# Input turned whole, one block of programs, and shifted half rows moved by DMA in a two-part attention kernel

## The reference

```
y = causal linear attention of layernorm(x)      # 16 heads of 8, rope, elu + 1
x = x + layernorm(y Wo)
z = layernorm(x)
for l in 0, 1:
    h = shift(z);  q, k, v = split(h wqkv[l])       # 8 heads of 64
    q, k = rope(l2norm(q) qs), rope(l2norm(k) ks)
    z = z + local_attention(q, k, v) wo[l]          # windows of 64, own and previous
    h = layernorm(shift(z)) g + b
    z = z + (a * gelu(g)) w2[l] + b2[l]             # a, g = split(h w1[l] + b1)
out = x + layernorm(z)

shift(t): features 0..63 of a token stay; features 64..127 come from the token before (0 for the first)
```

## Time and profile before

| | |
|---|---|
| median of 3 runs | 1832.37 us (1830.87 to 1837.6) |
| profiled execution | 1839.22 us |
| its span, first to last instruction | 1836.7 us |
| mean granted clock of TensorE | 0.971 |
| busy: PE, DVE, ACT, POOL | 1641.0, 1329.3, 1367.3, 1285.8 us |
| chain that ended last: PE, ACT, POOL, issue, DVE | 70, 12, 7, 6, 3 % |
| loads of x_in | issued at 35.7, 87.5, 172.7, 273.7, 377.9, ... 1523.3 us |

### The profile page before, as it was taken

One profiled execution on the slowest core, in us unless ns is written; L12 is line 12 of the kernel. 1 busy time (PEld: TensorE's weight loads), 2 busy tenths in 40 slices (PEclk: granted clock), 3 DMA queues, 4 the chain that ended last, 5 costly groups with the idle time before them and its releaser, 6 DMA issues.

```text
span 1836.7 us, 51372 instructions
## 1 busy us (share of the span) xinstructions
PE 1641.0 (89%) x18212; PEld 1149.2 (63%) x18340; DVE 1329.3 (72%) x3471; ACT 1367.3 (74%) x4277; POOL 1285.8 (70%) x1715
## 2 busy tenths in 40 slices
PE   0677989999999999999999999999999999998875
PEld 0344666666667666666666666666667666666653
DVE  2465777877777787877778787777777787776552
ACT  1264768787887878798887878787787878788663
POOL 1263777777777887777777787777777887777562
PEclk9888999999999999999999999999999999999986
DMA  3000001011111011111111011111101011111001
GB/s 117 12 16 19 22 23 25 18 36 30 36 28 28 19 34 27 31 36 30 36 28 28 19 31 30 31 36 28 39 22 31 22 25 36 30 31 30 19 21 29
DMA packets 58135, 54.52 MB, mean 30 GB/s; under 512 B 7538, under 2 KB 42780, under 8 KB 57756
## 3 DMA queue, kind: packets, MB, share of 16 engines
q1 hardware_dynamic: 57884, 51.25, 11.0%
HBM read 13.48 MB, written 8.39 MB: 12 GB/s over the span
## 4 chain that ended last, share of the span: by engine, by line
PE 70%; ACT 12%; POOL 7%; issue 6%; DVE 3%; DMA 0%; POOLq 0%; ACTq 0%; DVEq 0%; SPq 0%
PE bank L732 10%; PE bank L787 7%; PE bank L759 7%; PE bank L798 5%; PE bank L744 5%; PE bank L771 5%; PE bank L838 4%; PE bank L827 4%; PE bank L679 4%; PE bank L695 3%; PE bank L753 2%; PE bank L719 2%; ACT probs L959 2%; ACT probs_t L853 2%; POOL qk_rows L1308 2%
## 5 line engine op out<-in xcount | busy, mean ns | idle before, releaser
L959 ACT ACTIVATE probs<-bank,s_low 128x128 f32<-128x128 f32 x1024 | 360.1, 384 | 60.7 <-DVE s_low L1171 60.6
L1308 POOL TENSOR_TENSOR qk_rows<-qk_rows,qk_tmp 128x512 f32<-128x512 f32 x256 | 328.2, 1282 | 16.6 <-DVE qk_tmp L1159 15.8
L1321 POOL TENSOR_TENSOR probs<-probs,s_rden 128x512 f32<-128x512 f32 x256 | 263.5, 1050 | 68.1 <-DVE s_rden L1180 68.1
L732 PE MATMUL bank<-wqkv_sb,h_cols 128*128 128x512 f16 x1152 | 281.2, 388 | 7.9 <-ACT probs_t L853 2.6
L1311 POOL TENSOR_TENSOR qk_rows<-qk_rows,qk_rnorm 128x512 f32<-128x512 f32 x256 | 268.7, 1050 | 20.1
L959 ACT ACTIVATION_READ_ACCUMULATOR probs<-bank,s_low 128x1 f32 x1024 | 229.0, 224 | 0.0
L1156 DVE TENSOR_TENSOR qk_rows<-bank,rope 128x512 f32<-128x512 f32 x256 | 174.4, 681 | 39.2 <-POOL qk_rows L1311 35.4
L1126 DVE TENSOR_TENSOR room<-bank,const 128x512 f32<-128x512 f32 x256 | 158.7, 683 | 57.8 <-PE bank L679 56.2
L732 PEld LDWEIGHTS bank<-wqkv_sb,h_cols 128*128 128x128 f16 x1152 | 108.2, 99 | 142.7 <-issue 22.7
L853 ACT ACTIVATE probs_t<-bank 128x512 f32<-128x512 f32 x256 | 140.9, 598 | 67.9 <-PE bank L771 65.2
L1142 DVE TENSOR_REDUCE qk_sum<-qk_sq 128x16 f32<-128x1024 f32 x128 | 155.1, 1212 | 46.2 <-ACT qk_sq L918 44.2
(11 more groups left out here) (154 smaller groups left out, 3650.6 us busy)
## 6 DMA issues: line engine op xcount, KB each, us to landing
v_even<-v_rows SPq DMA_DIRECT2D x224, 128.0 KB, 2.3
x_in<-in_L_attn_x SPq DMA_DIRECT2D x16, 256.0 KB, 3.2
kept_rows<-x_in SPq DMA_DIRECT2D x16, 256.0 KB, 2.3
x_back<-kept_rows SPq DMA_DIRECT2D x16, 256.0 KB, 3.0
out<-x_back SPq DMA_DIRECT2D x16, 256.0 KB, 2.4
room<-in_constants SPq DMA_DIRECT2D x1, 1024.0 KB
hidden<-in_L_ffn_wqkv SPq DMA_DIRECT2D x1, 768.0 KB
qk_rows<-in_L_ffn_wqkv SPq DMA_DIRECT2D x1, 768.0 KB
```

What stands on the lines that cost most here:

```text
L732: mm = pe.matmul(to[:, :], h_cols[st.l][:, x_half, st.j * P:(st.j + 1) * P], wqkv_sb[:, st.l, w_half, w * INNER:(w + 1) * INNER], start=(n ...
L959: act.activation(probs[st.l][:, n, :], bank[b[half]][:, c * P:(c + 1) * P], ACT.Exp, bias=s_low[st.l][:, a, n:n + 1], accum_out=s_sum[st.l ...
L1308: pool.tensor_tensor(rows(w), rows(w), qk_tmp[l][:, w, :], ALU.add).then_inc(pool_qk.of(st), 1)
L1321: pool.tensor_tensor(probs[l][:, mine, :], probs[l][:, mine, :], s_rden[l][:, a, mine].unsqueeze(2).to_broadcast([P, PAIRS, P]), ALU.mult) ...
```

## The change

1. **h**: PE makes four whole transposes of 128 features. ACT and DVE each write in two instructions: partitions 0 to 63 straight, partitions 64 to 127 one column to the right. Column 0 of h_cols is set to zero once, at the start.
2. **sh**: the step leaves PE and DVE. SP issues two transfers within SBUF, from x_att to the right half of h2_rows: one for rows 0 to 126 of all tiles, and one for row 127 of tiles 0 to 2. ln_ffn sets the zero of token 0 and waits for them; b2 waits for them too. SP issues the step in its own order.
3. **One block**: x_in of batch 0 is loaded first, then the four small weights and the constants (first_loaded), then each layer's weights with a semaphore of its own. Splitting the weights and making the tables stand between steps of batch 0's linear attention on ACT and DVE. Each engine gives its own signals their first values. POOL clears smaller areas. The raw weights are held in other buffers until they are used.
4. **Tables**: STARTS, TIMES and HOLD are new throughout. A batch follows the one before by about 13,970 units.

```diff
-STARTS = [8839, 22968, 37104, 51237, ...]
+STARTS = [2215, 16195, 30174, 44135, ...]
 "tensor": {
-        "wo": [[23419, 23743, 26040, 28202], [45677, 46029, 48615, 48927]],
-        "sh": [[28994], [49311]],
-        "h2t": [[31502], [52223]],
+        "wo": [[23054, 23728, 25261, 26616], [44287, 45282, 45824, 47276]],
+        "h2t": [[30608], [52442]],
 "vector": {
-        "mask": [[10206, 11028, 15093, 15325]],
-        "wo": [[23817, 25113, 27959, 29115], [45566, 46809, 48074, 50301]],
-        "sh": [[29349], [50974]],
-        "ln_ffn": [[29524], [51038]],
+        "mask": [[9516, 10197, 13491, 13769]],
+        "wo": [[23238, 23893, 26482, 27433], [44992, 46277, 46648, 49255]],
+        "ln_ffn": [[28013], [50963]],
 "gpsimd": {
-        "pn": [[22629, 23612, 24629, 25752], [43947, 45525, 46189, 47917]],
-        "r_ffn": [[29895], [51024]],
-        "b2": [[29689], [53617]],
+        "pn": [[20891, 21929, 23937, 25173], [42109, 44911, 46038, 47508]],
+        "r_ffn": [[29262], [51986]],
+        "b2": [[27908], [52019]],
 "sync": {
-        "keep": [[15357]],
-        "v_up": [[21172, 25088, 25431, 25432], [42346, 42484, 46471, 46726]],
-        "v_down": [[22313, 25087, 27378], [41874, 43232, 46593]],
+        "keep": [[16331]],
+        "v_up": [[21510, 22278, 24351, 29331], [43527, 43686, 44265, 46405]],
+        "v_down": [[21488, 22864, 24850], [38817, 44910, 45864]],
+        "sh": [[29686], [49221]],
...
@@ SP
+                def shift(st):
+                    sp.wait_ge(*dve_wo.at(st.of("wo", NT - 1)))
+                    for l, n in ffn_turns(st):
+                        sp.wait_ge(*dve_h2t.at(Step("h2t", l, 0, n)))
+                    sp.dma_start(h2_rows[1:P, :, DH:D], x_att[st.l][0:P - 1, :, DH:D]).then_inc(sh_done.of(st), 16)
+                    sp.dma_start(h2_rows[0:1, 1:NT, DH:D], x_att[st.l][P - 1:P, 0:NT - 1, DH:D]).then_inc(sh_done.of(st), 16)
...
+                def load_first():
+                    for n, w in enumerate((wq, wk, wv, wo_la)):
+                        sp.dma_start(la_rows[:, n * D:(n + 1) * D], w).then_inc(first_loaded, 16)
+                    sp.dma_start(const[:, :], consts[:, 0:NCONST]).then_inc(first_loaded, 16)
...
+                start_signals(sp, ("x", "out", "v", "sh"))
+                for at, (_, st) in enumerate(order["sync"]):
+                    if at > 0:
+                        run(st)
+                        continue
+                    sp.dma_start(x_in[:, :, :], rows_of(x, st)).then_inc(x_loaded.of(st), 16)
+                    load_first()
+                    for l in range(DEPTH):
+                        load_layer(l)
+                    sp.wait_ge(zeroed, ZEROED)
@@ PE, h
-                    pe.matmul(to[DH:P, 0:1], ident[:, DH:P], cst("causal")[:, 0:1], start=True, stop=True)
                     for j in range(NT):
-                        n = min(P, T - 1 - j * P)
-                        pe.matmul(to[DH:P, j * P + 1:j * P + 1 + n], x_res[st.l][0:n, j, DH:D], ident[0:n, 0:n],
-                                  start=True, stop=True)
-                        mm = pe.transpose(to[0:DH, j * P:(j + 1) * P], x_res[st.l][:, j, 0:DH], ident)
+                        mm = pe.transpose(to[:, j * P:(j + 1) * P], x_res[st.l][:, j, :], ident)
@@ PE, sh
-                    pe.matmul(to[:, 0:NT * DH], cst("shift"), x_att[st.l][:, :, DH:D], start=True, stop=True)
-                    pe.matmul(to[0:1, DH:NT * DH], ident[:, P - 1:P], x_att[st.l][:, 0:NT - 1, DH:D],
-                              start=False, stop=True, skip_group_check=True).then_inc(pe_sh.of(st), 1)
@@ ACT, h
-                    copy(h_cols[st.l][:, 0, :], bank[b[0]][:, :]).then_inc(act_h.of(st), 1)
+                    copy(to[0:DH, 0, :], bank[b[0]][0:DH, :]).then_inc(act_h.of(st), 1)
+                    copy(to[DH:P, 0, 1:T], bank[b[0]][DH:P, 0:T - 1]).then_inc(act_h.of(st), 1)
@@ ACT, the steps
+                    if st.name() == ("av", 0, NT - 1, 0):
+                        halve(0)
+                    if st.name() == ("ao", 0, 0, 0):
+                        halve(1)
@@ DVE
                 def ln_ffn(st, b):
-                    dve.wait_ge(*dve_sh.at(st))
+                    for l, n in ffn_turns(st):
+                        dve.wait_ge(*dve_h2t.at(Step("h2t", l, 0, n)))
+                    dve.memset(h2_rows[0:1, 0, DH:D], 0.0).then_inc(dve_top.of(st), 1)
+                    dve.wait_ge(*sh_done.at(st))
                     dve.wait_ge(*act_h2x.at(st))
...
-                    dve.tensor_copy(h2_rows[:, :, DH:D], bank[b[0]][:, 0:NT * DH].rearrange(
-                        "p (j c) -> p j c", j=NT)).then_inc(dve_sh.of(st), 1)
...
+                turn_linear()
                 for _, st in order["vector"]:
+                    if st.kind == "rope" and st.n == 0 and st.j == 0:
+                        dve.wait_ge(ready[st.l], READY[st.l])
                     run(st)
+                    if st.name() == ("den", 0, 1, 0):
+                        lower_weights(0)
+                    if st.name() == ("mask", 0, 0, 0):
+                        turn_tables(0)
+                        turn_masks()
+                    if st.name() == ("mask", 0, 3, 0):
+                        lower_weights(1)
+                    if st.name() == ("ln_mid", 0, 0, 0):
+                        turn_tables(1)
@@ POOL, b2
-                    pool.wait_ge(*pe_sh.at(st))
+                    pool.wait_ge(*sh_done.at(st))
```

More of the change, by code:

```diff
@@ L126 @@
     },
     "vector": {
-        "ln_in": [[3336]],
-        "arope": [[4897, 5228, 5494, 7780]],
-        "phi": [[5339, 7394, 8144, 12251]],
-        "den": [[6519, 8903, 12441, 14291]],
-        "mask": [[10206, 11028, 15093, 15325]],
-        "ln_attn": [[15539]],
-        "norm_attn": [[16843]],
-        "ln_mid": [[17151]],
-        "h": [[18039], [38031]],
-        "ss": [[18745, 20244, 21725, 23553], [40963, 41947, 43215, 43739]],
-        "rope": [[19117, 21242, 22076, 22957], [41018, 42210, 43239, 44970]],
@@ L139 @@
[L139 to L148 removed]
+        "ln_in": [[2478]],
@@ new lines @@
+        "arope": [[4509, 4851, 5977, 7711]],
+        "phi": [[5537, 7658, 9024, 9514]],
+        "den": [[6686, 8534, 10335, 12072]],
+        "mask": [[9516, 10197, 13491, 13769]],
+        "ln_attn": [[14913]],
+        "norm_attn": [[15504]],
+        "ln_mid": [[16030]],
+        "h": [[16455], [37737]],
+        "ss": [[17547, 17941, 21041, 22184], [38308, 39081, 40943, 42320]],
+        "rope": [[17819, 18940, 21086, 22076], [38754, 40094, 41175, 43145]],
+        "max": [[21125, 21959, 22973, 24076], [41686, 43285, 43996, 44242]],
@@ L474, in build @@
[L474 removed]
+        whole_w1 = [of[:, :, :].rearrange("p h n -> p (h n)")[:, 0:2 * HID] for of in (probs[1], probs_t[1])]
+        qk_scale = qk_tmp[1][:, :, :].rearrange("p w n -> p (w n)")[:, 0:DEPTH * 2 * DH].rearrange(
             "p (l w c) -> p l w c", l=DEPTH, w=2)
[L476 removed]
+        first_loaded = ctx.enter_context(nc.semaphore("first_loaded"))
@@ new lines, in build, with start_signals @@
+        ready = [ctx.enter_context(nc.semaphore(f"weights_ready_{l}")) for l in range(DEPTH)]
+        FIRST_LOADS = 5
+        LOADS = [1 + 1 + 1 + 1 + 1 + 1 + 6 + 2 + 2 + (1 if l == 0 else 0) for l in range(DEPTH)]
+        ZEROED = 17
+        READY = [3 + 2 + 4 * NT + (3 if l == 0 else 0) for l in range(DEPTH)]
+        def start_signals(engine, mine):
+            for sig in every:
+                if sig.name.split("_")[0] in mine:
+                    for sem in sig.sems:
+                        engine.sem_inc(sem, sig.start())
@@ L568, in build @@
         pair_of = lambda t: t.rearrange("p (c n) -> p c n", c=PAIRS)
-        turns = [st for _, st in order["tensor"] if st.kind == "sh"]
+        turns = [st for _, st in order["sync"] if st.kind == "sh"]
         turn_at = {(st.l, st.n): at for at, st in enumerate(turns)}
@@ L615, in v_down @@
                     sp.dma_start(v_even[l][0:WIN, 1 - a, :], v_rows[l][WIN:P, a, :]).then_inc(v_low[st.j].of(st), 16)
-                does = {"load": load, "keep": keep, "bring": bring, "store": store, "v_up": v_up, "v_down": v_down}
+                def shift(st):
[4 more added lines that the diff above has]
+                    sp.dma_start(h2_rows[0:1, 1:NT, DH:D], x_att[st.l][P - 1:P, 0:NT - 1, DH:D]).then_inc(sh_done.of(st), 16)
@@ L619, in run @@
+                does = {"load": load, "keep": keep, "bring": bring, "store": store, "v_up": v_up, "v_down": v_down,
+                        "sh": shift}
                 def run(st):
                     does[st.kind](st)
-                for _, st in order["sync"]:
-                    run(st)
+                def load_first():
+                    for n, w in enumerate((wq, wk, wv, wo_la)):
+                        sp.dma_start(la_rows[:, n * D:(n + 1) * D], w).then_inc(first_loaded, 16)
+                    sp.dma_start(const[:, :], consts[:, 0:NCONST]).then_inc(first_loaded, 16)
@@ L1010, in _, with halve @@
```

(6 more changed lines are left out.)

315 lines of the change are left out of this document (154 added, 161 removed), and 25 rows, old and new, of tables (HOLD, TIMES).

## The result

The changed kernel takes 1922.55 us (median of 4 runs, 1921.77 to 1928.14) against 1834.4 us: ratio 1.0484, interval 1.0468 to 1.0499. The forecast was 1785 us. In the table of the experiments, two executions of e2_products at a much lower clock are left out of its time.

The account below looks back on a forecast made before the run. TensorE sets the 104.0 us steady period, forecast at 101.4; from a span of 1836.7 us, start -23, periods -38 and ends +14 give 1789.7, or 1785 us as measured time. Own range 1765 to 1808; 8 in 10: 1727 to 1830.

Parts of the forecast that it names:

- Step 1: TensorE, steady period: shorter h and no sh in both layers remove 5.9 us of its work per period.
- Step 2: ScalarE and VectorE, steady period: added copies stay hidden, 0.3 us of new idling, so 98.4 us if nothing else is late.
- Step 3: Shift transfer: one DMA engine, landing after 10.3 us; PE waits 3.0 us per period in layer 0, layer 1 hidden.
- Step 4: Start: x_in loaded first gains 29 us, put-off preparation inside batch 0 returns 6; net -23 us.
- Step 5: Fill and drain: the exposed landing of the transfer adds time, the shorter h gives back 2; sum +14 us.
- B: Rival: steady period does not follow TensorE's work, a further 2 us wait gives 103.5; 1816 us, chance 20%.
- A: Rival: many DMA engines share the shift, landing in 2.0 us inside the cover, period 98.4; 1727 us, chance 16%.
- C: Rival: one-engine transfer at its upper price, landing 15.4 us, period 106.8; 1876 us, slower, chance 12%.
- The test that I had named: Steady period: the forecast fails if PE's idle time per period grows by more than 6 us.

Follow-up runs that it names:

- e2_products: Changed kernel, new order, with the shift made again by two TensorE products and a VectorE copy instead of transfers: 1864.5 us (two runs).
- e4: Changed kernel with the order tables of the kernel before and the 127-row transfer cut into 112 and 15 rows: 1794.4 us.
- e17: Changed kernel with the 127-row transfer cut in two and norm_out moved on VectorE behind den(0) of batch n+4, ahead of ss(2): 1792.6 us.
- e16: Changed kernel with the old order and the cut transfer, final normalising done on one column of 128 only: 1792.8 us.
- e6: Kernel before with only the whole turn of h added, with its copies and subtractions in halves: 1820.8 us.
- e15: Changed kernel, new order, with the cut transfer, final normalising done on one column of 128 only: 1787.7 us.
- e11: Changed kernel with the old order and the cut transfer, ln_in of the next batch moved behind h and max on VectorE: 1874.4 us.
- e13: Changed kernel with the old order and the cut transfer, ln_in of the next batch moved directly behind h on VectorE: 1837.7 us.
- e14: Changed kernel with old order and cut transfer; in each first qkv step PE takes the products with the lower half of h last: 1804.8 us.
- e1: Changed kernel, new order, with only the 127-row transfer cut into 112 and 15 rows: 1829.2 us.
- e18: Changed kernel with the one-engine transfer kept and only norm_out moved, behind den(0) of batch n+4 on VectorE: 1895.0 us.
- e5: Changed kernel with the order tables of before and the shift by products and copy as before: 1799.6 us.
- e7: Changed kernel with the old order and the one-engine transfer, the shift's two issues exchanged so the small one goes first: 1987.8 us.

## Why the prediction was wrong

**Step 1, PE's work removed (5.9 us a period): the instructions went as forecast, the busy time fell by less, and the gain was smaller still.** From start to start h takes 0.53 us in e4 (0.46 forecast), and sh is gone. In e4 PE is busy 864.06/9 = 96.0 us. The 99.7 of the earlier trace rows are low: the trace of before lacks 88 of the 176 records of the mask products (L753) in that window, one of each pair. Set in like those of e17, they raise the busy time to 100.6 and lower the idle time from 4.3 to 3.4 (an estimate; the same done for e16, which lacks 72, gives 96.0, as e4 shows with none missing). So PE's busy time fell by 4.6 and not 5.9. Part of the rest is in the transposes of probs, which fill 82.9 us of nine periods in e4 and filled 78.2 before: they now stand behind waits. Of the 4.6 the period kept 1.7 in e4, and of 3.2 in e6 (busy 97.4 by the same estimate) 1.2.

**Step 2: this is the step that failed: "With less slack I add 0.3 us of new idling per period: 98.4 us if nothing else is late."** The work on ACT and DVE came out exactly (e4: 86.2 and 83.0; forecast 86.0 and 82.9), but with the landing out of the way the period is 106.5 in the new order and 102.4 in the old. Of the error of 9.3 us (110.7 against 101.4) 8.1 are in these 98.4 us, in two parts; all but the 1.3 to 1.9 us of busy time from step 1 are idle time and a lower clock, for which the step had 0.3.
- 3.7 us are the place of norm_out beside GpSimd's qk_rows: x_fin at 1197 ns instead of 338, a stand of PE of 2.2 us (1.9 us of idle time a period), and the clock behind it (1.8). e15 shows the cause by leaving the work out, e17 by moving it. I had said that I take no time from the new tables; I also took none from which engines they set beside each other.
- 4.4 us are left in the mended new order (e17: 102.8), 4.0 in the old (e4: 102.4). In e4 2.7 of them are idle time: PE stands 6.4 us a period where it stood 3.4, and I had allowed 0.3 more. The other 1.3 are the busy time of step 1. The waits listed for nine periods of before add up to 25 us without the stretch of missing records, those of e4 to 54. The largest is the lower half of h, 1.9 us a period. In both kernels DVE stands some 2.5 us at ln_in for x_in (21.3 and 23.4 us in nine periods); h(n)'s lower half stands behind it. Before, PE's own 2.49 us for h covered that; with h in 0.66 us it doesn't. DVE and PE around one such place, kernel before and then e4:

```profile
589.52 0.87 DVE L1027 BATCH_NORM_STATS2 ln_stats_in<-x_in 128x6 f32<-128x128 f32 x4 [2.62 <-DMA x_in<-in_L_attn_x]
591.19 0.69 DVE L1134 TENSOR_TENSOR h_cols<-bank,h_cols 128x512 f16<-128x512 f32 x1
587.96 0.28 PE L716 MATMUL bank<-const 128*64 128x1 f32 x2
591.25 2.37 PE L732 MATMUL bank<-wqkv_sb,h_cols 128*128 128x512 f16 x9
```

```profile
560.51 0.87 DVE L1005 BATCH_NORM_STATS2 ln_stats_in<-x_in 128x6 f32<-128x128 f32 x4 [2.55 <-DMA x_in<-in_L_attn_x]
562.75 0.69 DVE L1119 TENSOR_TENSOR h_cols<-bank,h_cols 64x511 f16<-64x511 f32 x1
559.03 0.66 PE L686 MATMUL bank<-const,x_res 128*128 128x128 f32 x4
563.50 1.69 PE L697 MATMUL bank<-wqkv_sb,h_cols 128*128 128x512 f16 x7 [1.59 <-DVE h_cols L1119]
```

e11, e13 and e14 moved this wait or changed its cover, and each came out slower; that it can't be moved away at all is not shown. That the arrival of x_in is what closes this loop is read from the traces and argued, not shown: a second x_in buffer would test it and was not tried.

**Step 3, the transfer: the mechanism was right and its size nearly so.** Landing 10.5 us after the first issue (forecast 10.3, plus 0.6 to the issue); POOL stands 5.8 us (4.6), DVE 3.2 (3.8), PE 3.2 (3.0); layer 1 hidden in the new order, as the 18 waits of DVE in 32 turns say. The packets show the one engine. In 5 us of the landing shown above 317 of them start, one each 16 ns, and their time is 7.8% of that of 16 engines, where one engine alone would be 6.3% (19.7 ns each, so neighbours overlap a little); in e1 all of them start within 2 us:

```profile
q1 hardware_dynamic: 317, 0.08, 7.8%
```

```profile
q1 hardware_dynamic: 545, 0.13, 31.8%
```

(DMA view of the kernel after, 446 to 451 us, and of e1, 132 to 134 us.) By the rule of the Trainium skill that the prediction cites (DMA: Bandwidth & Descriptors, "Why a DMA increments its semaphore by 16 and not by 1"), 127 rows go over one engine and 112 over sixteen; these rows and the landings of 10.5 us and under 3.7 agree with it. That the landing came so near to the forecast is in part luck: 508 packets at 16 ns are 8.0 us and not 8.9, and what is left beside them is 2.5 us and not 1.4. The term came to 4.2 us a period (110.7 less 106.5) and not 3.0: 3.1 us more idle time (27.5/9), and 1.2 because PE's 10.1 thousand instructions took 895.65 us instead of 885.10 at the lower clock, for which the prediction had no term. Counting the queue behind the shift at nothing was right in the changed kernel (v_even cost PE 1.7 us in nine periods), less so in e18 (8.6).

**Step 4, the start (-23): right.** ln_in at 10.02 us (8.5 to 10); the one block gives 21 us (e6 to e5), and the first b2 of e5 is at 133.8 us against 155.9 in e6.

**Step 5, the ends (+14): about +7.** The spans differ by 1920.0 - 1836.7 = 83.3 us; 14.6 x (110.7 - 104.0) = 98, less 22 for the start, leaves 7.

**The rivals.** B had the failing mechanism, a period that does not follow PE's work, and even its size (103.5 against the 102.8 of e17), but I weighed it as an alternative to the late landing; the two hold together. A's landing is e1's and e4's, and did not bring its 1727, since its base was the same 98.4. C's time (1876) was nearest to the result by the wrong mechanism: the landing was not 15.4 us. The test that I had named, idle time of PE growing by over 6 us a period, is what happened: from 4.3 (3.4 with the missing records) to 11.2.

## What to carry to other kernels

Taking work off the busiest engine is worth only what the loops beside it allow: 5.9 us of instructions removed took 4.6 off TensorE's busy time and brought 1.7 here, so list each wait of that engine that the removed work was covering (here the arrival of an input behind which a small step stood) before pricing it. Cut a transfer whose row count is like the 127 here, a prime, so that one DMA engine carries all of it, and when an order is made anew, look at which VectorE instructions with all operands in SBUF it sets beside long GpSimd ones. Look at the clock behind a stand of TensorE (2.2 us cost 3.7 here), and time a new order and a new transfer apart as well as together: this order was worth 44 us with the late transfer and cost 35 without it.

## What the hardware showed that I had not expected

- The issue that follows the 508-packet transfer on SP takes 6.92 to 7.04 us in the kernel after (32 of 32), against 0.5 to 0.8 in the rows around it. In e7 another transfer takes its place: where it follows within 1 us (16 times) it takes 6.82 to 6.92 us, and where it comes over 16 us later, 0.5. In e1 the issue behind the 15-row piece takes 0.74 to 0.75 us.
- Four x_fin instructions took 1.17 us where GpSimd was nearly idle (e17) and 4.1 beside its 128x512 operations (after). There the second, third and fourth begin at 937.79, 938.91 and 940.15 us, 0.01 us behind the ends of GpSimd's first three (936.51 + 1.27, 937.86 + 1.04, 938.86 + 1.28), while those keep the durations that they have elsewhere (1270 and 1066 ns in the mean of all 256). The Trainium skill (SBUF — State Buffer, "SBUF: two separate sides") says that VectorE in a two-port mode and GpSimd take one pair of ports in turn, for a whole instruction; the rows agree in that VectorE waited for the end of GpSimd's instructions and alone was the slower; in which mode VectorE ran they do not show.
- The length of a stand of PE does not tell whether the granted clock falls behind it. It fell to 0.61 and 0.69 for some 4 us after stands of 2.2 us (e1, after), and to 0.58 after one of 1.58 us (e1); it stayed 1.00 after one of 1.88 us (e1) and after one of 3.25 us (e4). In nine periods before has no stand over 1.2 us and e4 eight, with the clock at 1.00 throughout; e1 has 18 and a mean of 0.98. What decides is open. PE's stand and its window, e1 and then e4:

```profile
1204.89 1.68 PE L697 MATMUL bank<-wqkv_sb,h_cols 128*128 128x512 f16 x5 [1.58 <-DVE h_cols L1119]
1204.89:1209.00 4.11, 4.11 (x16) 0.58 0.15 32
```

```profile
872.03 1.68 PE L697 MATMUL bank<-wqkv_sb,h_cols 128*128 128x512 f16 x7 [3.25 <-DVE h_cols L1119]
872.00:876.00 4.00, 3.84 (x21) 1.00 0.00 0
```
